# Sums of a graph layer: four neighbouring node tiles in one PSUM bank, instead of one chained add per step

## The reference

```python
h = x @ W_enc.T + b_enc
row, col = (edge_index[0], edge_index[1])          # src, dst
for l in range(n_layers):                          # 2 layers
    m = jnp.concatenate([h[row], h[col]], axis=-1)
    m = jax.nn.relu(m @ msg_W1[l].T + msg_b1[l])
    m = m @ msg_W2[l].T + msg_b2[l]
    agg = jax.ops.segment_sum(m, col, num_segments=h.shape[0])
    upd = jnp.concatenate([h, agg], axis=-1) @ upd_W[l].T + upd_b[l]
    h = _layer_norm(h + upd, ln_g[l], ln_b[l])
return h @ W_out.T + b_out
```

## Time and profile before

| what | us |
|---|---|
| median of 3 runs | 3997.04 |
| lowest, highest | 3991.55, 3998.21 |
| profiled execution, first to last instruction (span) | 3444.6 |
| median less span | 552.4 |
| PE busy in the span | 2975.2 (86%) |
| PEld busy | 2674.1 (78%) |
| DVE busy | 2700.0 (78%) |
| ACT busy | 2379.7 (69%) |
| POOL busy | 1846.0 (54%) |

### The profile page before, as it was taken

One profiled execution on the slowest core, in us unless ns is written; L12 is line 12 of the kernel. 1 busy time (PEld: TensorE's weight loads), 2 busy tenths in 40 slices (PEclk: granted clock), 3 DMA queues, 4 the chain that ended last, 5 costly groups with the idle time before them and its releaser, 6 DMA issues. The chain is left out here.

```text
span 3444.6 us, 92529 instructions
## 1 busy us (share of the span) xinstructions
PE 2975.2 (86%) x25312; PEld 2674.1 (78%) x25312; DVE 2700.0 (78%) x8634; ACT 2379.7 (69%) x5642; POOL 1846.0 (54%) x1782
## 2 busy tenths in 40 slices
PE   4975656777767789997999998999979999989998
PEld 3753334555543378987999998999979999989998
DVE  9999967888856688885777776666657777769998
ACT  3779945777742368886777775666657777759999
POOL 0000036577755533335776776555547767766664
PEclk9999988999979989999999999999989999999999
DMA  0027635777649989997776654999977766548887
GB/s 21 2 69 229 223 103 162 221 219 215 195 139 340 346 280 355 366 356 250 225 221 208 191 158 123 327 327 326 328 239 229 221 210 194 164 129 287 296 295 240
DMA packets 460711, 777.79 MB, mean 226 GB/s; under 512 B 113689, under 2 KB 115865, under 8 KB 460393
## 3 DMA queue, kind: packets, MB, share of 16 engines
q1 hardware_dynamic: 355046, 548.85, 48.2%
q10 hardware_dynamic: 67714, 147.73, 12.5%
q0 software_dynamic: 37632, 77.15, 9.2%
HBM read 451.50 MB, written 321.78 MB: 224 GB/s over the span
## 5 line engine op out<-in xcount | busy, mean ns | idle before, releaser
L883 DVE SCALAR_TENSOR_TENSOR edges_acc<-edges_acc,keep,edges_ps_a 128x128 f32 (+1 forms) x2352 | 820.3, 349 | 272.1 <-issue 145.9
L851 POOL DMA_INDIRECT ring<-table_p,esrc x784 | 787.5, 1004 | 313.3 <-issue 206.0
L1011 PE MATMUL edges_ps_m<-ring,ident 128*128 x3136 | 609.7, 276 | 33.8 <-POOLq L840 33.8
L1012 PE MATMUL edges_ps_m<-edges_q_ring,edges_turned 128*128 x3136 | 608.8, 276 | 0.0
L1011 PEld LDWEIGHTS edges_ps_m<-ring,ident 128*128 128x128 f32 x3136 | 478.6, 193 | 34.7 <-ACT edges_turned L967 17.7
L1012 PEld LDWEIGHTS edges_ps_m<-edges_q_ring,edges_turned 128*128 128x128 f32 x3136 | 478.8, 193 | 0.0
L979 ACT ACTIVATE edges_msg<-edges_ps_m 128x512 f32<-128x512 f32 x392 | 234.2, 597 | 295.5 <-PE edges_ps_m L1012 294.7
L1021 PE MATMUL edges_ps_a<-edges_onehot,edges_msg 128*128 128x128 f32 x3136 | 414.0, 275 | 0.0
L851 POOL DMA_INDIRECT ring<-table_h,esrc x344 | 327.7, 953 | 138.5 <-issue 93.5
L1021 PEld LDWEIGHTS edges_ps_a<-edges_onehot,edges_msg 128*128 128x128 f32 x3136 | 381.7, 192 | 0.0
L868 DVE TENSOR_TENSOR edges_onehot<-iota,drel 128x512 f32<-128x512 f16 x441 | 305.0, 692 | 96.1 <-PE edges_ps_a L1021 94.0
(11 more groups left out here) (315 smaller groups left out, 6776.2 us busy)
## 6 DMA issues: line engine op xcount, KB each, us to landing
table_z<-nodes_z_t SPq DMA_DIRECT2D x196, 256.0 KB, 5.0
table_p<-nodes_p_out SPq DMA_DIRECT2D x196, 256.0 KB
table_q<-nodes_q_out ACTq DMA_DIRECT2D x196, 256.0 KB
edges_q_ring<-table_q SPq DMA_DIRECT2D x196, 256.0 KB, 4.8
edges_d_ring<-table_d ACTq DMA_DIRECT2D x98, 512.0 KB
table_t<-edges_acc SPq DMA_DIRECT2D x196, 256.0 KB
nodes_in_a<-table_t SPq DMA_DIRECT2D x196, 256.0 KB
nodes_in_z<-table_z SPq DMA_DIRECT2D x196, 256.0 KB, 4.3
```

The source lines that it names most:

```text
L851: nc.gpsimd.indirect_dma_start(out=ring[:, e % RE * W:e % RE * W + P], out_offset=None, in_=table[:, :], in_offset=bass.IndirectOffsetOnAx ...
L883: nc.vector.scalar_tensor_tensor(out=to, in0=to, scalar=m.keep[:, s:s + 1], in1=ps_a[:, i % AR, where(j):where(j) + F], op0=ALU.mult, op1= ...
L1011: nc.tensor.matmul(to, m.ident[:], rows[j], start=True, stop=False)
L1012: last = nc.tensor.matmul(to, turned[:, i % QR, j * P:(j + 1) * P], slots[j], start=False, stop=True)
```

## The change

`edge_stage` now serves only the stage of the convolution and is what it was there. The two layers have a stage of their own, `message_stage` (line 1009 of the changed kernel). In it:

- `ADDED` = 3: of the four gathered rows of a batch only the fourth is added by PE with the identity (line 1214). The other three are added by DVE into `ps_m`, behind the combination (`add_rows`, line 1125). ACT's message waits for it (`s_add`), and POOL's gathers do too, instead of for `s_pq`.
- The four products of `segment` (line 1231) accumulate in one bank of `ps_a`, whose quarters are now the four neighbouring node tiles from the batch's first on. The quarter comes from a register, out of a new table `wins`. Only the first product starts the bank. Steps of the same node tile thus add up in PSUM.
- DVE moves the first of the four tiles with one operation, carried tile * keep + sum (`move`, line 1136); ACT copies the other three (`copy`, line 1178) behind it. `move(i)` waits for `copy(i-1)`, PE's segment of batch i for `copy(i-3)`, and the store of SP for `s_copied`.
- `acc` has three spare tiles on either side of the ring's end (`SPARE`), so that three tiles can be copied across it. Every eighth chunk is therefore stored in four pieces. The three banks of `ps_a` are cleared at the start.
- DVE's order is move(i-2), loads and one-hot of i+1, rows of i. ACT's is turn(i+2), copy(i-2), message(i). PE's stays.
- Tables `spots` (two words per batch, loaded by DVE and ACT every four batches), `added` (four words per batch, loaded by DVE every two), `wins` (loaded by PE every four), `where` and `batch_end` (SP) are new and made in the plan stage.

```diff
@@ plan_stage, ahead of the rows that TensorE waits for @@
                 nc.vector.memset(ends[:], 1)
+                nc.vector.memset(ended_in, -1)
+                nc.vector.memset(m.spots[:], 0)
+                nc.vector.memset(m.added[:], 0)
+                nc.vector.memset(m.batch_end[:], 0)
...
                 dve.sem_inc(s_rows, 1)
+
+                link(nc.vector.tensor_copy(ended_in[:, 3:3 + TP], sen_row[0:1, 1:1 + TP]))
...
+                for k in range(3):
+                    link(nc.vector.tensor_tensor(m.where[:], m.where[:], same[:, k, :], ALU.add))
...
                 dve.wait_ge(s_cols, 1)
...
@@ plan_stage, the packed tables @@
-                link(nc.vector.tensor_scalar(ik(5), ik(1), 2, None, ALU.arith_shift_right))
...
-                link(nc.vector.tensor_scalar(ik(8), ik(5), 1, None, ALU.add))
...
-                pack(table[:, :, 1], 5, [of(8, 3)] + [of(3, j) for j in range(4)], 7)
+                reach = ik(8)[:, 0:NB]
...
+                pack(table[:, :, 1], 5, [reach] + [of(3, j) for j in range(4)], 7)
+                for j in range(1, J):
+                    done = nc.vector.scalar_tensor_tensor(out=far[:, j - 1, :], in0=of(1, 0), scalar=-1.0, in1=of(1, j), op0=ALU.mult, op1=ALU.add)
...
+                nc.vector.tensor_scalar(spots[:, 0:NB, 1], of(3, 0), float(P), None, ALU.mult)
+                link(nc.vector.tensor_tensor(far[:, 2, :], far[:, 2, :], of(3, 0), ALU.add))
+                nc.vector.tensor_scalar(spots[:, 1:NB, 0], far[:, 2, 0:NB - 1], float(P), None, ALU.mult)
+                for j in range(ADDED):
+                    done = nc.vector.tensor_scalar(added[:, 0:NB, j], of(2, j), float(W), None, ALU.mult)
...
-                for k, to in ((0, m.chunk_end), (3, m.tile_end)):
+                for k, to in ((0, m.chunk_end), (3, m.tile_end), (4, m.batch_end)):
...
@@ message_stage, in place of edge_stage for the layers @@
+                def store(c, tiles, at):
+                    to = turn_back(c) * P
+                    sp.dma_start(agg[to:to + P, tiles[0] * P:(tiles[-1] + 1) * P], acc[:, at]).then_inc(s_out[c % 2], 16)
...
+                    if c % RC == 0 and c:
+                        spots = loaded(nc, mybir.EngineType.SP, m.where[0:1, c * J:c * J + SPARE], S - 1)
+                    sp.wait_ge(s_copied, third(ends, c) if c < NCHUNK - 1 else NB)
+                    if c % RC == 0 and c:
+                        for j in range(SPARE):
+                            store(c, [j], bass.ds((spots[j] % J + SPARE - j) // J * (4 * RC * P) + j * P, P))
+                        store(c, [SPARE], slice(SPARE * P, CH))
+                    else:
+                        store(c, range(J), slice(at * CH, (at + 1) * CH))
...
+                        pool.wait_ge(s_add, third(ends, k))
...
+                nc.vector.memset(acc[:], 0.0).then_inc(s_zero, 1)
+                for b in range(QR):
+                    nc.vector.memset(ps_a[:, b, :], 0.0).then_inc(s_zero, 1)
...
+                def fetch(i):
+                    if i % 4 == 0:
+                        word["spots", i // 4 % 2] = loaded(nc, mybir.EngineType.DVE, m.spots[0:1, 2 * i:2 * i + 8], (4 * RC + SPARE - 1) * P)
+
+                    if i % 2 == 0:
+                        word["rows", i // 2 % 2] = loaded(nc, mybir.EngineType.DVE, m.added[0:1, 4 * i:4 * i + 8], (RE - 1) * W)
+
...
+                def hot(i):
+                    if i >= HR:
+                        dve.wait_ge(s_seg, i - HR + 1)
+                    nc.vector.tensor_tensor(onehot[:, i % HR, :, :], m.iota[:, 0:P].unsqueeze(1).to_broadcast([P, 4, P]),
+                                            m.drel[:, 4 * i:4 * i + 4].unsqueeze(2).to_broadcast([P, 4, P]), ALU.is_equal).then_inc(s_hot, 1)
+
+                def add_rows(i):
+                    rows = [ring[:, bass.ds(row_at(i, j), P)] for j in range(ADDED)]
+                    for at in rows:
+                        nc.vector.lower_ap(at)
+                    dve.wait_ge(s_pq, i + 1)
+                    for j in range(ADDED):
+                        last = nc.vector.tensor_tensor(tile(ps_m, i, j), tile(ps_m, i, j), rows[j], ALU.add)
+                    last.then_inc(s_add, 1)
+
+                def move(i):
+                    carried, first = (acc[:, bass.ds(spot(i, k), P)] for k in range(2))
+                    for at in (carried, first):
+                        nc.vector.lower_ap(at)
+                    dve.wait_ge(s_seg, i + 1)
+                    if i >= 1:
+                        dve.wait_ge(s_win, i)
+                        dve.wait_ge(s_copied, i)
+                    nc.vector.scalar_tensor_tensor(out=first, in0=carried, scalar=m.keep[:, 4 * i:4 * i + 1], in1=tile(ps_a, i, 0),
+                                                   op0=ALU.mult, op1=ALU.add).then_inc(s_win, 1)
+
+                fetch(0)
+                hot(0)
+                for i in range(NB + BEHIND):
+                    if i >= BEHIND:
+                        move(i - BEHIND)
+                    if i + 1 < NB:
+                        fetch(i + 1)
+                        hot(i + 1)
+                    if i < NB:
+                        add_rows(i)
...
+                def copy(i):
+                    if i % 4 == 0:
+                        word[0] = loaded(nc, mybir.EngineType.Activation, m.spots[0:1, 2 * i:2 * i + 8], (4 * RC + SPARE - 1) * P)
+                    others = acc[:, bass.ds(word[0][i % 4 * 2 + 1] + P, CH - P)]
+                    nc.scalar.lower_ap(others)
+                    act.wait_ge(s_win, i + 1)
+                    nc.scalar.copy(others, ps_a[:, i % QR, P:CH]).then_inc(s_copied, 1)
+
+                for g in range(DR - 1):
+                    load_drel(g)
+                turn(0)
+                turn(1)
+                for i in range(NB):
+                    if i + 2 < NB:
+                        turn(i + 2)
+                    if i >= BEHIND:
+                        copy(i - BEHIND)
+                    act.wait_ge(s_add, i + 1)
+                    if i >= QR:
+                        act.wait_ge(s_seg, i - QR + 1)
+                    nc.scalar.activation(msg[:, i % QR, :], ps_m[:, i % QR, :], ACT.Relu).then_inc(s_msg, 1)
...
+                def combine(i):
+                    if i % 2 == 0:
+                        word[0] = loaded(nc, mybir.EngineType.PE, m.steps[0:1, 2 * i:2 * i + 4])
+                    k = i % 2 * 2
+                    landed = [nc.tensor.compute_val(word[0][k + u] & 127) for u in range(2)]
+                    rows = {j: ring[:, bass.ds(word[0][k] // (1 << (7 + 6 * j)) % 64 * W, P)] for j in range(ADDED, J)}
+                    slots = [q_ring[:, bass.ds(word[0][k + 1] // (1 << (7 + 5 * j)) % 32 * P, P)] for j in range(J)]
+                    for at in [*rows.values(), *slots]:
+                        nc.tensor.lower_ap(at)
+                    pe.wait_ge(s_turned, 2 * i + 2)
+                    pe.wait_ge(s_prow, landed[0])
+                    pe.wait_ge(s_n, landed[1])
+                    for j in range(J):
+                        if j >= ADDED:
+                            nc.tensor.matmul(tile(ps_m, i, j), m.ident[:], rows[j], start=True, stop=False)
+                        last = nc.tensor.matmul(tile(ps_m, i, j), tile(turned, i, j), slots[j], start=j < ADDED, stop=True)
+                    last.then_inc(s_pq, 1)
+
+                def segment(i):
+                    if i % 4 == 0:
+                        spots[0] = loaded(nc, mybir.EngineType.PE, m.wins[0:1, i:i + 4])
+                    to = [tile(ps_a, i, 0)] + [ps_a[:, i % QR, bass.ds(spots[0][i % 4] // (1 << (2 * j - 2)) % J * P, P)] for j in range(1, J)]
+                    for at in to[1:]:
+                        nc.tensor.lower_ap(at)
+                    pe.wait_ge(s_hot, i + 1)
+                    pe.wait_ge(s_msg, i + 1)
+                    if i >= QR:
+                        pe.wait_ge(s_copied, i - QR + 1)
+                    else:
+                        pe.wait_ge(s_zero, 2 + i)
+                    for j in range(J):
+                        last = nc.tensor.matmul(to[j], tile(msg, i, j), onehot[:, i % HR, j, :], start=j == 0, stop=True, skip_group_check=True)
+                    last.then_inc(s_seg, 1)
```

377 lines of the change are left out of this document (203 added, 174 removed).

## The result

The changed kernel takes 4108.82 us (median of 4 runs, 4088.36 to 4116.75) beside 3994.30 of the kernel before: a ratio of 1.0282, interval 1.0253 to 1.0312. It is slower by 2.8%, outside the range and on the other side of the forecast.

The account below looks back on a forecast made before the run. PE was taken to bound the message stages at 2.68 us per batch, POOL close behind. Batches of 2.6 make a stage 524 us, 35 off in both; plan stage +8; 3997 - 27 = 3970 us, range 3922 to 4040.

Parts of the forecast that it names:

- The step that failed: Whole kernel: 552 us between the trace's span of 3444.6 and the median of 3997.04 lie around it, left unchanged.
- PE binds: Message stages of the kernel before: PE busy nearly all the time, 2.68 us per batch, POOL close behind.
- The batch: Changed message stages: 2.6 us per batch, between 2.4 (loop through ACT and DVE) and 2.84 (PE's instruction issue).
- Rival D: Message stages: PE's instruction issue makes the batch 2.80 us, stage 563, time 4048; chance 0.21.
- POOL: Message stages: same 392 gathers at a pitch of 1.30, 520 us; release 0.7 us later, covered by the ring.
- root error: Message stages: forecast wrong if POOL waits for row adds in the second half; then DVE and ACT set the pace.
- Rival B: Message stages: gathers unhindered by DVE's compare, pitch 1.245, stage 499, time 3920; chance 0.13.
- The plan stage: Plan stage, ended by DVE: added memsets and operations for the new tables cost +8 us (5 to 11).
- Copy, adds, loads: Message stages, per batch: ACT's copy 0.48 us, DVE's three row adds 0.68, a load of 8 words 0.63.
- Rival E: Loop through DVE: a table load costs 1.27 us, batch 2.92, time 4095; with 1.6 per load 4185; chance 0.03.

Follow-up runs that it names:

- r2: Kernel before with no gathers in its two message stages, POOL only reporting all groups as landed; ratio 0.9038 to the kernel before.
- r1: Kernel before run again with no edit, for a second trace; span 3981.7 us beside a time of 3983.4, ratio 1.0010.
- r3: Changed kernel with no gathers in its two message stages, POOL only reporting all groups as landed; ratio 0.8934 to the kernel before.
- r4: Changed kernel with all four gathered rows added by PE, none by DVE, and table `added` neither made nor loaded; 4031 us, ratio 1.0106.
- r16: Changed kernel with POOL at most 8 groups ahead and a memset on POOL behind every second gather; 3927 us, ratio 0.9914.
- r17: Kernel before with DVE's four chained adds one batch earlier in the message stages (i-2 instead of i-3); ratio 0.9994.
- r10: Changed kernel with DVE's move and ACT's copy one batch later (i-3 instead of i-2); 4069 us, ratio 1.0218.
- r13: Changed kernel with all four gathered rows added by PE and the move and copy one batch later; ratio 1.0137.
- r7: Kernel before with a POOL memset, waited for, behind every second gather of the message stages; 3932 us, ratio 0.9851.

## Why the prediction was wrong

**The step that failed** is the one with no working: "552 us lie around it up to the median of 3997.04, and I leave these as they are". They were inside. They are the holds beside gathers: without the gathers of the message stages the kernel before falls by 384 us (r2), and the convolution's edges stage and the plan stage, which also gather, take 597 and 94 us from PE's first to its last weight load in r1 instead of 466 and 57. All rows of the sum came from an execution that no timed run resembles, and "PE binds" was true of it alone. Where there are no holds, the forecast fits: without gathers the changed kernel is 42 us faster than the kernel before (r3 and r2), where 27 were forecast.

**Point by point.** *The batch.* Forecast 2.6 us, between 2.4 and 2.84; without gathers it is 2.59. The size was right, the reason probably not: I took it for PE's issue, and the waits of r3 point to the loop through ACT, which I had put at 2.4. *Rival D*, slower by PE's issue, was of the right sign with the wrong mechanism: it would show without gathers, and there the changed kernel is faster. *POOL.* Forecast: gathers of 1.30 bind the stage, and their later release costs nothing "since POOL is seldom late at its wait". In truth POOL waits 242 us for the row adds, since PE's results come late. What the prediction named as its root error happened: POOL waits for the row adds. *Rival B*, gathers unhindered by the compare: the compare does lengthen them, in r1 too (1.26 at 2006.04, beside the one-hot of 2005.79), so the rows stood and the rule did not. *The plan stage.* Forecast +8, 5 to 11; from r1 to the changed kernel the edges stage's first weight load moves from 583.8 to 589.2, +5. *Copy, adds, loads.* ACT's copy takes 0.465 (0.48 forecast), three row adds 0.69 to 0.70 (0.68), a load of eight words 0.60 (0.63). *Rival E*: its estimate with 1.6 us for a load is 4193 by its own terms, not 4185; with 0.60 measured nothing rests on it.

**What took the place of the gain.** Per batch the kernel before needs PE's results in two places that stand side by side: the message on ACT behind the combination, and the one-hot and chain on DVE behind the sums. In the changed kernel DVE stands behind both (row adds and move), ACT behind DVE twice (message and copy), and PE behind ACT: each late result of PE can stop all three. DVE in the changed kernel at the start of a message stage:

```profile
1783.66 0.69 DVE L1125 TENSOR_TENSOR edges_ps_m<-edges_ps_m,ring 128x128 f32<-128x128 f32 x3 [15.20 <-issue]
1804.72 0.35 DVE L1136 SCALAR_TENSOR_TENSOR edges_acc<-edges_acc,keep,edges_ps_a 128x128 f32 x1 [20.36 <-issue]
```

It is held by the one, then by the other. r4 takes DVE out of the first and gives back 1.8 of the 2.8%; r16 makes the holds short and gives back all. That the late results cost the 2.8% is shown by r16. That it is their number in a row which makes the changed order lose more is argued: it fits r4 and r17, but the little that r10 gained speaks for the lag as well; and what keeps the last 1% in r13 was not separated into copy, tables and order. The clock plays a small part. The granted clock in this stage is 0.82, where it was 0.90 in r1, and a matmul of line 1231 lasts 310 ns in the mean where line 1021 takes 285 in r1. But PE is busy for 511 us instead of the 443 of r3 in the changed kernel and for 590 instead of the 529 of r2 in the kernel before: 68 and 61 us more, so by my estimate at most 7 of the 60 us are the clock's.

## What to carry to other kernels

Compare the span of a profile with the time of the runs before anything else; where they differ by more than a few us, the trace shows another execution than the one that is timed, and no term may be taken from it until a second trace agrees. Beside long series of indirect gathers, break the series (and, as far as r4 shows it, keep TensorE's results off the paths of engines that are waited for): pauses after every second gather took 1.5% off a kernel whose gathers were early anyway. Leave enough lookahead with it: with 4 groups the same pauses cost 8%. Measure an edit once without the suspected disturber (r2, r3): it tells in one run whether the edit or its surroundings lose.

## What the runs showed of the hardware

While POOL issues gathers one after another, results of PE reach other engines late in the timed executions: 1.44 us in the median, mostly in bursts of four and eight, and 0.04 where a 0.54 us memset stands behind every second gather (r7). In an unbroken series of 64 only two batches get through in 80 us, with matmuls 1.4 to 3.5 us apart. The one execution ahead of the prediction had series of up to 204 gathers and every message 0.04 us after PE, so more than the gathers is needed, and what that is no run shows. The amount of data is no part of it (16 instead of 512 bytes per row: ratio 1.0012). DVE's handoffs to ACT stay at 0.03 us beside the same gathers, and the node stages, which gather nothing, are alike in all traces (399 us, from first to last weight load, in both executions of the kernel before).

The Trainium skill, SBUF — State Buffer, section Who interferes with whom, has one rule of contention, the port pair of VectorE and GpSimd, and says that PE and ACT never wait on anyone. It speaks of the ports of SBUF, and no run shows whether PE's lateness comes by a port. For ACT the 0.03 agrees; whoever reads the sentence as a promise that PE is free of what GpSimd does is put right by the runs. The same section reasons, marked as inferred, that a two-input tensor_tensor leaves descriptor generation alone; that isn't borne out: in r1 the 53 gathers of the first message stage that begin within a compare last 1.24 us in the median, those beside other work of DVE or none 0.94. The section's rule that two SBUF inputs contend with a GpSimd instruction that reads SBUF would agree, since a gather takes its row numbers (`esrc`) from there.
